# A four-stage graph and mixture-of-experts kernel: row gathers issued further ahead, landings awaited later, and the combination moved into the experts' block

## The reference

```python
# L0: 64 experts, two per row, at most 78 rows each; L3: 8 experts, two per row, at most 250 rows each
x2 = layernorm(x + attention(layernorm(x)))
gate, idx = top_k(softmax(x2 @ wr), 2)
h = gelu(rows_of_expert @ w1[e] + b1[e])
y = h @ w2[e] + b2[e]
out = x + gate[0] * y[idx[0]] + gate[1] * y[idx[1]]
# L2: 8 experts, the best one per row, all its rows
G, idx = max(softmax(xt @ Wr + br)), argmax
y = G * (relu(xt @ W1[idx] + b1[idx]) @ W2[idx] + b2[idx])
```

## Time and profile before

| | us |
|---|---|
| median of 3 runs | 3631.22 (3630.07 to 3634.32) |
| the profiled execution | 3633.83 |
| its span in the profile | 3631.7 |
| TensorE busy | 2808.2 (77%) |
| VectorE busy | 1685.9 (46%) |
| ScalarE busy | 944.7 (26%) |
| POOL busy | 288.2 (8%) |
| mean granted TensorE clock | 0.85 of full |

### The profile page before, as it was taken

One profiled execution on the slowest core, in us unless ns is written; L12 is line 12 of the kernel. 1 busy time (PEld: TensorE's weight loads), 2 busy tenths in 40 slices (PEclk: granted clock), 3 DMA queues, 4 the chain that ended last, 5 costly groups with the idle time before them and its releaser, 6 DMA issues. The chain is left out here.

```text
span 3631.7 us, 41563 instructions
## 1 busy us (share of the span) xinstructions
PE 2808.2 (77%) x12659; PEld 1981.1 (55%) x12660; DVE 1685.9 (46%) x3356; ACT 944.7 (26%) x2087; POOL 288.2 (8%) x273
## 2 busy tenths in 40 slices
PE   5888879958999766676738759977867679998673
PEld 3555546546777444444516436665644457775542
DVE  6776631247888342222233453242122458884332
ACT  1222210024777300010111112220101237774100
POOL 0000000000000012222200000000220000001031
PEclk9999989978999857777769889996988789998676
DMA  3000052010000145555341230004323110000333
GB/s 95 0 0 0 12 152 53 2 55 20 21 20 11 38 133 165 166 168 169 122 112 31 117 79 14 12 4 146 120 58 84 40 31 21 20 17 8 92 106 102
DMA packets 113514, 237.87 MB, mean 65 GB/s; under 512 B 32500, under 2 KB 33860, under 8 KB 112130
## 3 DMA queue, kind: packets, MB, share of 16 engines
q10 hardware_dynamic: 44810, 121.37, 11.1%
q1 hardware_dynamic: 44280, 87.26, 8.6%
q0 software_dynamic: 24320, 27.90, 2.7%
HBM read 189.78 MB, written 52.58 MB: 67 GB/s over the span
## 5 line engine op out<-in xcount | busy, mean ns | idle before, releaser
L1042 DVE TENSOR_REDUCE mx<-ps 125x1 f32<-125x500 f32 (+1 forms) x480 | 274.0, 589 | 56.7 <-PE ps L812 40.8
L243 PE MATMUL ps<-onehot_src,onehot_dst 125*128 x1200 | 258.0, 354 | 41.4 <-DVE onehot_dst L219 15.9
L937 ACT ACTIVATE probs_hi<-ps 125x500 fp32r<-125x500 f32 (+1 forms) x480 | 254.9, 531 | 123.6 <-DVE probs_lo L994 80.4
L218 DVE TENSOR_SCALAR onehot_src<-iota,src_f 125x1250 f16 x400 | 217.8, 545 | 109.3 <-PE ps L243 96.3
L1655 DVE COPY yb<-ps 78x512 f32<-78x512 f32 (+1 forms) x100 | 68.8, 688 | 406.8 <-PE ps L1602 406.8
L939 ACT ACTIVATE x<-ps 125x500 f32<-125x500 f32 (+1 forms) x480 | 257.6, 537 | 0.0
L994 DVE TENSOR_TENSOR probs_lo<-x,probs_hi 125x1250 fp32r<-125x1250 f32 x160 | 240.9, 1506 | 35.2 <-ACT x L939 31.7
L1602 PE MATMUL ps<-w2s,hT 128*78 128x512 f32 (+1 forms) x480 | 238.4, 647 | 0.0
L1621 ACT ACTIVATE hT<-ps,b1s 128x78 f32<-128x78 f32 (+1 forms) x240 | 67.5, 343 | 590.1 <-PE ps L1593 589.9
L243 PEld LDWEIGHTS ps<-onehot_src,onehot_dst 125*128 x1200 | 121.0, 102 | 172.0 <-issue 116.8
L1593 PE MATMUL ps<-xbT,room 128*128 128x78 f32 (+1 forms) x1280 | 205.6, 337 | 0.5 <-issue 0.5
(11 more groups left out here) (366 smaller groups left out, 5017.9 us busy)
## 6 DMA issues: line engine op xcount, KB each, us to landing
room<-in_L_ffn_w_p ACTq DMA_DIRECT2D x72, 512.0 KB, 5.9
w2s<-in_L_ffn_w ACTq DMA_DIRECT2D x72, 512.0 KB, 6.9
G<-c_spill ACTq DMA_DIRECT2D x2, 5859.4 KB
tv<-in_L_ffn_tv_W_p SPq DMA_DIRECT2D x2, 4096.0 KB
w1s<-in_L_ffn_w_p ACTq DMA_DIRECT2D x8, 1024.0 KB, 4.9
w2s<-in_L_ffn_W ACTq DMA_DIRECT2D x8, 1024.0 KB, 9.4
Y<-expert_rows SPq DMA_DIRECT2D x15, 480.0 KB
w_spill<-W SPq DMA_DIRECT2D x5, 1171.9 KB
```

The source lines that it names most:

```text
L218: v.tensor_scalar(ohs[:, slot, :].rearrange("p o n -> p (o n)"), io16[:, 0:N], sF[:, bass.ds(tile, 1)], None, ALU.is_equal)
L243: mm_ = pe.matmul(ps[:, 3 * half + c, 0:cn], ohd[:, slot, :].rearrange("p o n -> p (o n)"), ohs[:, slot, c0:c0 + cn].rearrange("p o n -> p ...
L937: act.activation(PH[:, t % 2, c0:c0 + cn], ps[0:P, ST + n, 0:cn], ACT.Exp, scale=SCALE).then_inc(p_hi, 1)
L1042: v.tensor_reduce(mx[:, t, n:n + 1], ps[0:P, SQ + cc % 2, 0:cn], AX.X, ALU.max)\
```

## The change

- POOL gathers four units ahead instead of two (`DEEP` = `RING` = 4), `yb` keeps two slots (`YDEEP`) with their own `stored` semaphores, and the landing of a unit's scatters is awaited after the next unit's scatters were issued. L2 stays one deep.
- The refills of the weight ring are issued by SP, not ACT.
- The bias products and their additions stand after the last unit. `combine` is gone as a block: its loads wait for the semaphore `all_stored` and write into `res` and `yn` (`xn` in L2), no longer into a tile of their own.
- The residual is added in `route`, while VectorE waits for positions; x is reloaded by ACT (`later`, semaphore `x_back`).
- In `route` the gates come before the slots on VectorE.
- Semaphores are cleared by ranges. `expert_rows` has no spare rows any more (writes beyond 2N were dropped already).

```diff
     def clear_semaphores(self, nc):
-        todo, self.used_semaphores = self.used_semaphores, []
+        numbers, self.used_semaphores = sorted({s.num for s in self.used_semaphores}), []
...
-                for s in todo:
-                    pool.sem_clear(s)
+                for first, end in runs:
+                    pool.sem_clear(range(first, end))
...
                     v.tensor_copy(M16[:, :, :], OH[:, 0, :, :]).then_inc(masks, 1)
+                if meanwhile is not None:
+                    meanwhile(v)
                 v.wait_ge(pos_done, 1)
...
-                v.wait_ge(slots_done, 1)
-                s.did(v.tensor_copy(slots[0:R, 0, :], ps[0:R, 1, 0:NB]))
...
+                v.wait_ge(hots, 2 * topk)
...
+                v.wait_ge(slots_done, 1)
+                s.did(v.tensor_copy(slots[0:R, 0, :], ps[0:R, 1, 0:NB]))
...
-    DEEP = 1 if dynamic else 2
+    DEEP = 1 if dynamic else RING
+    YDEEP = 1 if dynamic else 2
...
-                def landed(u):
+                def landed(u, slot, times):
                     for s in range(2):
-                        pool.wait_ge(stored[s], u * 16 + 16)
+                        pool.wait_ge(stored[slot][s], times * 16)
                         pool.sem_inc(yb_free[s], 1)
...
-                    gather(1, 1)
                     for u in range(UNITS):
-                        if u + 2 < UNITS:
+                        if u + DEEP < UNITS:
                             emptied(u)
-                            gather(u + 2, u % 2)
-                        scatter(u, u % 2)
-                        landed(u)
+                            gather(u + DEEP, u % DEEP)
+                        scatter(u, u % YDEEP)
+                        if u:
+                            landed(u - 1, (u - 1) % YDEEP, (u - 1) // YDEEP + 1)
+                    landed(UNITS - 1, (UNITS - 1) % YDEEP, (UNITS - 1) // YDEEP + 1)
+                pool.sem_inc(all_stored, 1)
+
+            def loads(eng, c):
+                eng.wait_ge(all_stored, 1)
+                src = rowtiles(y_dram[c * N:c * N + N, :])
+                for h in range(PIECES):
+                    for to, what in in_two(Y[c][:, TP * h:TP * h + TP, :], src[:, TP * h:TP * h + TP, :]):
+                        eng.dma_start(to, what).then_inc(got[h], 16)
+
+            @block.sync
+            def _(sp):
+                def weights(i, g):
+                    sp.wait_ge(w_used[g], i + 1)
+                    wts.issue(sp, i, g)
...
+                weights(ROUNDS - 1, RING - 1)
+                loads(sp, 0)
...
-                for t in range(T):
-                    if t >= 2:
-                        pe.wait_ge(bias_taken, t - 1)
-                    pe.matmul(ps[0:P, BIAS[t % 2], :], r.gateT[:, P * t:P * t + P], b2, start=True, stop=True)\
-                        .then_inc(bias_summed, 1)
...
                 run_ahead(pe, turn, products, after=lambda g: pe.drain().then_inc(w_used[g], 1))
+                for t in range(T):
+                    if t >= 2:
+                        pe.wait_ge(bias_taken, t - 1)
+                    pe.matmul(ps[0:P, BIAS[t % 2], :], r.gateT[:, P * t:P * t + P], b2, start=True, stop=True)\
+                        .then_inc(bias_summed, 1)
...
                         hidden_at(i, g)
-                weights(ROUNDS - 1, RING - 1)
...
+                if K_ == 2:
+                    loads(act, 1)
...
+                run_ahead(v, affine_rows, take)
                 for t in range(T):
                     v.wait_ge(bias_summed, t + 1)
...
-                if res is not None:
-                    v.wait_ge(bias_taken, T)
-                    v.tensor_tensor(x[:, :, :], x[:, :, :], res[:, :, :], ALU.add)
-                run_ahead(v, affine_rows, take)
...
         norm_rows(nc, k, res, yn, xnT, (g2, b2), have_stats=True,
-                  beside=in_two(x, rowtiles(x_spill)) + [(b2r[:, :], a[pre + "b2"]), (wr[:, :, :], kchunks(a[pre + ("router_w" if bias else "wr")]))]
+                  later=[(to, what, x_back) for to, what in in_two(x, rowtiles(x_spill))],
...
+            def add_residual(v):
+                v.wait_ge(x_back, 32)
+                v.tensor_tensor(x[:, :, :], x[:, :, :], res[:, :, :], ALU.add)
```

More of the change, by code:

```diff
@@ L327, in clear_semaphores @@
     def clear_semaphores(self, nc):
-        todo, self.used_semaphores = self.used_semaphores, []
+        numbers, self.used_semaphores = sorted({s.num for s in self.used_semaphores}), []
+        runs = []
+        for n in numbers:
+            if runs and runs[-1][1] == n:
+                runs[-1][1] = n + 1
+            else:
+                runs.append([n, n + 1])
         with nc.Block() as block:
@@ L1475, in both @@
                 def both(i, u, g):
[L1476 removed]
+                    ahead(u, u + 1, 0, 0, True)
                     body(i, u, g, 0)
@@ L1491, in steps @@
                     after(g)
-            ahead(0, 1, 0, False)
+            ahead(0, 1, 0, 0, False)
             with eng.Fori(0, ROUNDS - 1) as i:
@@ L1540, in _ @@
                 for s in range(2):
-                    pool.sem_inc(yb_free[s], DEEP)
-                gather(0, 0)
+                    pool.sem_inc(yb_free[s], YDEEP)
+                for u in range(DEEP):
+                    gather(u, u)
                 if dynamic:
@@ L1606, in _ @@
                 run_ahead(pe, turn, products, after=lambda g: pe.drain().then_inc(w_used[g], 1))
+                for t in range(T):
+                    if t >= 2:
+                        pe.wait_ge(bias_taken, t - 1)
+                    pe.matmul(ps[0:P, BIAS[t % 2], :], r.gateT[:, P * t:P * t + P], b2, start=True, stop=True)\
+                        .then_inc(bias_summed, 1)
             @block.scalar
             def _(act):
-                def weights(i, g):
-                    act.wait_ge(w_used[g], i + 1)
-                    wts.issue(act, i, g)
                 def hidden_at(i, g):
@@ L1870, in transformer @@
         x = x128[0:P]
-        x_out = ctx.enter_context(k.semaphore(nc, k.name("x_out")))
+        x_out, x_back = (ctx.enter_context(k.semaphore(nc, k.name(n))) for n in ("x_out", "x_back"))
         Gf = sb(ctx, "room", [128, T, N])
@@ L2417, in program @@
         c_out = ctx.enter_context(k.semaphore(nc, "c_out"))
-        UNUSED = 64 * 78
-        rows_dram, y_dram = scratch("rows", (N, D)), scratch("expert_rows", (2 * N + UNUSED, D))
+        rows_dram, y_dram = scratch("rows", (N, D)), scratch("expert_rows", (2 * N, D))
         x_spill, sums_dram = scratch("x_spill", (N, D)), scratch("sums", (2, N))
```

96 lines of the change are left out of this document (39 added, 57 removed).

## The result

The changed kernel takes **3323.71 us** (median, 3323.14 to 3324.77), against 3630.64 for the kernel before in the same measurements: the ratio is 0.9154, 95% interval 0.9138 to 0.9170. The prediction was 3317 in a range of 3290 to 3385, on its way a profiled execution of 3320 where the one measured is 3324.28 (span 3322.5). So 309 us of span went; 314 were forecast.

The account below looks back on a forecast made before the run. The prediction took POOL's wait for its own scatters to land as the brake, leaving TensorE idle, then at half clock. Its terms summed to -314 us: 3633.8 to 3320 profiled, 3317 as a median, range 3290 to 3385.

Parts of the forecast that it names:

- Term 1: L0 loop (64-expert mixture): rows ready four units ahead, so a unit takes 8.06 us at full clock; -201.5 us.
- The covers: L0 loop, per 8.06 us unit: POOL issues 5.1 us, landing 2.5 to 7.9 us, DMA 7.8 us, the thinnest.
- Rival A: L0 loop: the DMA engines bind at 9.7 us a unit; +36 us, 3353 us; chance 0.15.
- Term 2: Start of L0's block: first unit waits for gathers, no longer for bias products; -14.9 us (L3 -15, L2 -11).
- Term 3: Routing: gates before the slots lie beside products or transposition; -4.4 us in L0, -2.9 in L3, -1.5 in L2.
- Term 4: Norm block and routing: x reloaded by ScalarE's queue; +1.5 us in L0 (between -4.9 and +6), -5.4 in L3.
- Term 5: Seven blocks clearing 304 semaphores: ranges leave 24 instructions; -19.0 us.
- Term 6: End of the mixtures' blocks: Y loads no longer wait for POOL's closing DRAIN; -10.6 (L0), -2.8 (L3), -0.5 us (L2).
- Rival C: End of block: the DRAIN is owed before the semaphore is seen; +13.5 us, 3331 us; chance 0.07.
- Term 7: L3 loop, eight units: 70.4 us instead of 96.1, a warm unit 8.35 us; -25.7 us.
- Rival B: TensorE's clock: pausing every unit, it falls to 0.50, a unit say 12 us; +126 us, 3443 us; chance 0.07.
- Rival E: POOL's single queue: landings over 30.7 us make the kernel slower; 3685 us at a landing of 34; chance 0.02.

Follow-up runs that it names:

- n_unrolled: The changed kernel with the loops over units in L0 and L3 written out on ScalarE and TensorE; 3315.11 us.
- e_more_bytes: The changed kernel with 1 MB more copied from DRAM to DRAM behind each L0 unit's weight refill; 3344.87 us.
- e_two_ahead: The changed kernel with rows gathered two units ahead instead of four, the landing still awaited a unit later; 3405.2 us.
- e_at_once: The changed kernel with POOL waiting for a unit's scatters to land right behind them, rows still gathered four units ahead; 3345.85 us.
- e_x_in_norm: The changed kernel with x reloaded by SP inside the norm block, which waits for it, as before; 3338.17 us.
- n_best: The changed kernel with unit loops written out, L2's table read by TensorE before its first unit, and five of ten bias products ahead of the first unit; 3312.45 us.
- e_combine_apart: The changed kernel with the loads and additions of Y in a block of their own behind the experts' block; 3350.3 us.

## Why the prediction was right

- **Term 1, the L0 loop**: -195.0 where -201.5 was forecast. The mechanism was right, and the unit 8.08 instead of 8.06 us. Missing was about 1 us at each of seven turns of the loop, some 6 to 7 us (n_unrolled); the trace of before shows them only where a unit does not wait for rows anyway. The Trainium skill (DMA: Bandwidth & Descriptors, "Measured") gives 6.15 us for a transfer of 1 MB and, in the same row, 341 GB/s. By the time, which the prediction took, the loop would have stayed as slow as it was; by the rate, an estimate from the page, a unit's 2.55 MB take 7.5 us. The traces disagree with the first and bear out the second: 296 GB/s over the changed loop, 376 in e_more_bytes.
- **The reason given for it** named both parts in one breath. The runs separate them: depth is the larger part, and the later landing alone leaves 2 us of pause in every other unit.
- **The covers**: POOL's 5.1 us of issues and the landing were covered. The DMA cover, called the thinnest, was about 1.7 us by e_more_bytes and not 0.3 (8.06 less 7.8). By the prediction's own measure the changed loop has 0.89 x 8.34 = 7.4 us; shares of packets that overlap count more than the bytes do. Rival A was priced on the right mechanism and was not due.
- **Term 2, start of L0**: -14.3 for -14.9; L3 -14.6 for -15. **L2** is the miss: -7.8 for -11, and +1.8 at its end for -0.5. "Now about 10" was L0's 12.0 made shorter without a row behind it; it is 13.2 us from the block's start, 1.1 of it POOL's copy of the unit's rows and the pause behind that, ahead of the first gather. And "if they run at half clock about 5 us show" was said of L0, and happened in L2, where TensorE's products were not enough ahead of Y.
- **Term 3, gates**: -6.1 (L0), -3.4 (L3), -1.6 (L2) for -4.4, -2.9, -1.5. In L0 the transposition of the gates now follows the slots' products after 0.28 us instead of 5.07, and takes 1.26 us instead of 2.29, at full clock.
- **Term 4, reload of x**, is the step that failed: -14.7 in all for +1.5 - 5.4 = -3.9, outside its own bounds in L0 (-7.0 against -4.9). The text saw ScalarE queue its weights behind x, and gave back what the norm block won; the exponentials came 2.4 us earlier after the routing's start, not later. In absolute time the table load came 7.0 us earlier (1285.82 for 1292.78), though x was issued 3.2 us later. The DMA engines, busy for 0.41 of the time from 1272 to 1276 in the kernel before, were busy for all of it now, with the weights right behind x; that this is the whole cause was not tested. In the other kernels that keep the reload on ScalarE L0's routing up to the positions won 1.2 to 2.6 us, beside about 4.7 of the norm block, so L0's part is outside the bound in each of them. Another 2.4 of the 14.7 us are L3's logits at full clock at their start, which the text did not see either. They came in four of twelve such kernels, so in the changed kernel they are luck.
- **Term 5, clears**: -16.8 for -19.0; 4.3 us remain for seven blocks, 2.9 of them the 24 range clears, which the sum took as dear as single ones.
- **Term 6, DRAIN**: -10.7 and -2.9 for -10.6 and -2.8. Rival C fell: the loads went out 0.04 us ahead of a DRAIN as long as before. L3 gave 1.9 us back behind the loads of Y; no run tells why.
- **Term 7, L3 loop**: -30.4 for -25.7: the first unit there was taken as cold (12.4 us and the restart) and took 9.3, which is most of it. The earlier trace rows already showed its first products at 5.63 us, not at the 7.04 of half clock.
- **Rival B** did not come in the changed kernel, but it is what e_two_ahead shows, every second unit. **Rival E** never came near: landings took 3.2 to 7.2 us (1400 to 1580 us).

Summed over the three mixtures, the terms came out at -195.0 (forecast -201.5), -36.7 (-40.9), -11.1 (-8.8), -14.7 (-3.9), -16.8 (-19.0), -9.4 (-13.9), -30.4 (-25.7) and +0.4 for L2's loop, together -313.7 where -314 was forecast. That is closer than the terms deserve, and luck: the misses lie on both sides and cancel. The 4.5 us that are left are stretches that the change does not touch.

## What to carry to other kernels

A loop that alternates between waiting and half clock pays twice, so the first 2 us of pause removed are worth more than their length (in e_two_ahead a pause of 2.2 to 2.9 us in every second unit costs about 6 us); work out from the trace how late the data are, in units, before choosing a depth. In a short loop a stream that is slower than the engine it feeds may cost little, if it starts some units ahead (e_at_once). When a wait is covered, write down by what: here two improvements that hid under the same wait were worth less together than their sum.

## What the runs showed of the hardware

- TensorE's clock: idle times of 2.21 us (e_two_ahead), 6.98 (before) and 7.66 us (e_x_in_norm) were followed by products at half clock; those of 0.79 and 0.69 us (e_at_once) and of 2.36 us between L0's norm block and its logits were not. The length of the last pause alone does not decide it: waits of 0.99 and 0.98 us in e_at_once stood ahead of first products of 6.40 us; in L2 of the changed kernel a pause of 1.97 us was followed by first products of 9.04 us and one of 1.95 us by 7.41; L0's logits took 8.91 us behind 2.36 us in the changed kernel and 14.58 behind 2.44 in n_best; and L3's logits behind 2.3 us took 20.0 us in four kernels and 22.4 in eight.
- POOL's closing DRAIN lasted 10,510, 2,667 and 466 ns in L0, L3 and L2 of the changed kernel and of e_combine_apart, to the nanosecond as before. The blocks have 128, 32 and 40 indirect DMAs, so the length does not follow their number; what sets it stays open.
- A loop on ScalarE loads its activation table again at each turn (1.28 us, seven times in L0), and once, ahead of the first unit, where the loop is written out (n_unrolled).
- A read of a table value by TensorE costs about 0.5 us, an estimate: 16 of them lie in the 8.04 us that TensorE idles in n_best.
